# Second half's mixing matmuls: x and block diagonal split into high and low parts, three fp32r products for each fp32 one, one pair later

## The reference

```python
w = table[cond]                                   # 32 matrices of 32 x 32
y = einsum('bct,bcd->bdt', x, w)                  # mixing, per batch
h = silu(y @ w_gate) * (y @ w_up)                 # 1024 x 1024
h = keep_the_two_largest_of_each_four(abs(h), h)  # 2:4 sparsity, by magnitude
out = x + h @ w_down
```

## Time and profile before

| | us |
|---|---|
| median of three runs | 80.29 |
| profiled execution, its own time | 80.31 |
| its span | 78.4 |
| PE busy | 73.9 (94%) |
| DVE busy | 62.7 (80%) |
| ACT busy | 42.1 (54%) |
| share of PE in the chain that ended last | 94% |

### The profile page before, as it was taken

How to read it: one execution, slowest core, us unless ns; L and a number is a source line. 1 busy time by engine, 2 the same in 40 slices (tenths; PEclk the granted TensorE clock), 3 DMA queues, 4 the chain that set the end, 5 groups by cost and what they waited for, 6 DMA issues and landing times.

```text
span 78.4 us, 1027 instructions
## 1 busy us (share of the span) xinstructions
PE 73.9 (94%) x362; PEld 59.6 (76%) x362; DVE 62.7 (80%) x93; ACT 42.1 (54%) x62; POOL 8.1 (10%) x17
## 2 busy tenths in 40 slices
PE   3988999999999999999999999999999999999950
PEld 1328888888888888888888888888888888888840
DVE  1006884689889999599999979999999999994460
ACT  6122773799443465699897769798380402720000
POOL 3460000000000013000804000006200000000000
PEclk9999999999999999999999999999999999999999
DMA  0726979995910005900199990003994000003333
GB/s 1 273 95 168 286 234 318 302 418 180 410 67 0 0 0 98 169 0 0 36 196 199 184 192 8 4 0 67 201 180 88 0 0 0 8 0 140 135 134 126
DMA packets 4565, 9.64 MB, mean 123 GB/s; under 512 B 560, under 2 KB 2864, under 8 KB 4304
## 3 DMA queue, kind: packets, MB, share of 16 engines
q1 hardware_dynamic: 3488, 6.16, 23.0%
q0 software_dynamic: 928, 3.28, 21.9%
q10 hardware_dynamic: 144, 0.13, 0.5%
HBM read 5.38 MB, written 1.05 MB: 82 GB/s over the span
## 4 chain that ended last, share of the span: by engine, by line
PE 94%; issue 1%; DVE 1%
PE banks L579 52%; PE banks L621 28%; PE banks L541 6%; PE banks L564 4%; PE banks L591 3%; PE banks L550 1%; DVE gate_raw L455 1%; DVE warm L458 0%
## 5 line engine op out<-in xcount | busy, mean ns | idle before, releaser
L579 PE MATMUL banks<-y_hl,up_hl 128*128 128x512 f32 x96 | 24.2, 389 | 0.0
L621 PE MATMUL banks<-h_hl,down_hl 128*128 128x512 f32 (+1 forms) x102 | 22.0, 376 | 0.0
L579 PE MATMUL banks<-y_hl,gate_hl 128*128 128x512 f32 x84 | 21.4, 390 | 0.0
L621 PEld LDWEIGHTS banks<-h_hl,down_hl 128*128 128x128 f32 x102 | 18.5, 188 | 3.6
L579 PEld LDWEIGHTS banks<-y_hl,up_hl 128*128 128x128 f32 x96 | 18.0, 188 | 3.8
L579 PEld LDWEIGHTS banks<-y_hl,gate_hl 128*128 128x128 f32 x84 | 15.7, 188 | 3.2
L264 ACT ACTIVATE silu<-banks 128x512 f32<-128x512 f32 x16 | 9.6, 597 | 11.1 <-PE banks L579 10.8
L404 DVE TENSOR_TENSOR h<-banks,silu 128x512 f32<-128x512 f32 x12 | 8.2, 687 | 3.8 <-ACT silu L264 3.7
L285 ACT ACTIVATE h_hl<-h 128x1024 fp32r<-128x1024 f32 (+1 forms) x8 | 6.7, 842 | 3.9 <-DVE h L440 3.9
L440 DVE SCALAR_TENSOR_TENSOR h<-count,h 128x512 f32<-128x512 bf16 x12 | 7.9, 685 | 0.1
L271 ACT ACTIVATE x_sb<-h 128x512 f32<-128x512 f32 x8 | 4.9, 625 | 1.7 <-DVE h L404 1.7
(11 more groups left out here) (39 smaller groups left out, 66.7 us busy)
## 6 DMA issues: line engine op xcount, KB each, us to landing
h_hl<-h POOLq DMA_DIRECT2D x4, 512.0 KB, 6.1
x_sb<-in_x SPq DMA_DIRECT2D x2, 512.0 KB, 3.7
up_raw<-in_w_up SPq DMA_DIRECT2D x4, 256.0 KB, 4.3
down_raw<-in_w_down SPq DMA_DIRECT2D x1, 1024.0 KB, 7.6
gate_raw<-in_x_t SPq DMA_DIRECT2D x1, 1024.0 KB, 5.9
down_hl<-down_raw POOLq DMA_DIRECT2D x2, 512.0 KB, 4.9
gate_raw<-in_w_gate SPq DMA_DIRECT2D x3, 256.0 KB, 4.1
out<-gate_raw SPq DMA_DIRECT2D x3, 256.0 KB, 2.3
```

The lines of the kernel that those rows point to most:

```text
L579: last = nc.tensor.matmul(dst, w_hl[w][:, s, q, k, j], y_hl[:, m, half, k], start=i == 0, stop=i == len(terms) - 1)
L621: last = nc.tensor.matmul(bank[:, begin:end], down_hl[:, s, q, j, k * P:(k + 1) * P], h_hl[:, u, m, j, begin:end], start=(q, j, m, s) == f ...
```

## The change

The second half's x (128 x 1024) and its block diagonal (128 x 512) are each split into a high and a low fp32r part: ACT copies the high parts (`high_x`, `high_diagonal`), DVE subtracts to get the low parts (`low_x`, `low_diagonal`). They are kept in the part of `h_hl` that belongs to the last unit, which is written only near the end. `mixing_second_half` takes the place of `mixing(1)`: for each block and group three fp32r matmuls of 128 columns that add up in one bank, 24 in all where there were 8 of fp32. It stands ahead of pair 4, one pair later. `transpose_rows(1)` and `diagonal(SPANS[2])` move ahead of product(0) on DVE, and `high_y` and `low_y` of the second half stand behind `gate_silu(3)` and `product(3)`. The first half's mixing is as before, written as a function of its own.

```diff
--- before.py
+++ after.py
@@ -36,7 +36,7 @@
     RING = 3
     WARM_START = 12
     LAST = len(UNITS) - 1
-    MIX_PAIR = 3
+    MIX_PAIR = 4
     SENT = 2
 
 
@@ -76,6 +76,10 @@
         mix_w = h[:, 1, 1, 0:NG * D].rearrange("p (g o d) -> p g o d", o=1, d=D)
         mix_diag = h[:, 1, 2:4].rearrange("p m t -> p (m t)").rearrange(
             "p (g b d) -> p g b d", g=NG, b=NB)
+
+        last_h = h_hl[:, LAST].rearrange("p s m t -> p (s m t)")
+        x_hl = last_h[:, 0:2 * GH * T].rearrange("p (s g t) -> p s g t", s=2, g=GH)
+        diag_hl = last_h[:, 2 * GH * T:2 * GH * T + 2 * GH * P].rearrange("p (s g n) -> p s g n", s=2, g=GH)
         own_block = sb("own_block", [P, NB], f32)
         far = sb("far", [P, 4, TH], bf16)
         near = sb("near", [P, 2, TH], bf16)
@@ -117,6 +121,8 @@
         blocks_marked = sem("blocks_marked")
         transposed = sem("transposed")
         diag_done = sem("diag_done")
+        second_hi = sem("second_hi")
+        second_lo = sem("second_lo")
         mixed = sem("mixed")
         y_hi = sem("y_hi")
         y_lo = sem("y_lo")
@@ -177,6 +183,9 @@
         def parts_until(u, j):
             return sum(len(p) for p in PARTS[:u]) + 1 + max(i for i, p in enumerate(PARTS[u]) if p[0] <= j)
 
+        def second_diag():
+            return mix_diag[:, GH:NG].rearrange("p g b d -> p g (b d)")
+
         def raw_piece(i):
             q, w, k, end, j, j_end = PIECES[i]
             return raw_w[w][:, q, k:end].rearrange("p k (j g) -> p k j g", j=M)[:, :, j:j_end]
@@ -257,6 +266,14 @@
                 act.wait_ge(mixed, KT * half + end)
                 nc.scalar.activation(split_y(HI, half, k, end), mixed_y(half, k, end), ACT.Copy).then_inc(y_hi, 1)
 
+            def high_x():
+                act.wait_ge(x_in[1], 16)
+                nc.scalar.activation(x_hl[:, HI], x_sb[:, GH:NG], ACT.Copy).then_inc(second_hi, 1)
+
+            def high_diagonal():
+                act.wait_ge(diag_done, len(SPANS))
+                nc.scalar.activation(diag_hl[:, HI], second_diag(), ACT.Copy).then_inc(second_hi, 1)
+
             def gate_silu(n):
                 act.wait_ge(pair_done, n + 1)
                 if n >= 3:
@@ -298,15 +315,17 @@
                 high_weights(i)
             act.wait_ge(table_loaded, 1)
             gate_silu(0)
+            high_x()
             gate_silu(1)
+            high_diagonal()
             absolute(0)
             high_weights(LATER)
             gate_silu(2)
             absolute(1)
             high_weights(LATER + 1)
-            high_y(*Y_PIECES[KT])
             absolute(2)
             gate_silu(3)
+            high_y(*Y_PIECES[KT])
             absolute(3)
             gate_silu(4)
             gate_silu(5)
@@ -380,6 +399,18 @@
                 nc.vector.tensor_tensor(mix_diag[:, groups], mix_w[:, groups].broadcast_to(shape),
                                         mark.broadcast_to(shape), ALU.mult).then_inc(diag_done, 1)
 
+            def low_x():
+                dve.wait_ge(second_hi, 1)
+                dve.wait_ge(x_in[1], 16)
+                nc.vector.tensor_tensor(x_hl[:, LO], x_sb[:, GH:NG], x_hl[:, HI].bitcast(f32),
+                                        ALU.subtract).then_inc(second_lo, 1)
+
+            def low_diagonal():
+                dve.wait_ge(second_hi, 2)
+                dve.wait_ge(diag_done, len(SPANS))
+                nc.vector.tensor_tensor(diag_hl[:, LO], second_diag(), diag_hl[:, HI].bitcast(f32),
+                                        ALU.subtract).then_inc(second_lo, 1)
+
             def low_weights(i):
                 dve.wait_ge(w_hi, i + 1)
                 dve.wait_ge(*source(i))
@@ -467,16 +498,18 @@
                 low_y(k)
             for i in range(KT, LATER):
                 low_weights(i)
-            product(0)
-            product(1)
             transpose_rows(1)
             diagonal(SPANS[2])
+            product(0)
+            low_x()
+            product(1)
+            low_diagonal()
             low_weights(LATER)
             product(2)
             compare(0, 1)
             low_weights(LATER + 1)
+            product(3)
             low_y(KT)
-            product(3)
             compare(0, 2)
             compare(0, 3)
             product(4)
@@ -551,20 +584,27 @@
                                                 mix_w[rows, g, 0], start=True, stop=True)
                 last.then_inc(mixed, 1)
 
-            def mixing(half, first=0):
-                pe.wait_ge(x_in[half], 16)
-                if half > 0:
-                    pe.wait_ge(y_lo, KT * half)
-                for k in range(first, KT):
-                    for i in range(GH):
-                        g = half * GH + i
-                        span = [groups.start <= g < groups.stop for groups in SPANS].index(True)
-                        if k == first and g == SPANS[span].start:
-                            pe.wait_ge(diag_done, span + 1)
-                        last = nc.tensor.matmul(y_banks[:, k, i * P:(i + 1) * P],
-                                                x_sb[:, g, k * P:(k + 1) * P],
-                                                mix_diag[:, g].rearrange("p b d -> p (b d)"),
-                                                start=True, stop=True)
+            def mixing_second_piece():
+
+                for g in range(GH):
+                    span = [groups.start <= g < groups.stop for groups in SPANS].index(True)
+                    if g == SPANS[span].start:
+                        pe.wait_ge(diag_done, span + 1)
+                    last = nc.tensor.matmul(y_banks[:, 1, g * P:(g + 1) * P], x_sb[:, g, P:2 * P],
+                                            mix_diag[:, g].rearrange("p b d -> p (b d)"), start=True, stop=True)
+                last.then_inc(mixed, 1)
+
+            def mixing_second_half():
+
+                terms = ((HI, HI), (HI, LO), (LO, HI))
+                pe.wait_ge(second_lo, 2)
+                pe.wait_ge(second_hi, 2)
+                pe.wait_ge(y_lo, KT)
+                for k in range(KT):
+                    for g in range(GH):
+                        for s, m in terms:
+                            last = nc.tensor.matmul(y_banks[:, k, g * P:(g + 1) * P], x_hl[:, s, g, k * P:(k + 1) * P],
+                                                    diag_hl[:, m, g], start=(s, m) == terms[0], stop=(s, m) == terms[-1])
                     last.then_inc(mixed, 1)
 
             def split_product(dst, w, q, half, j):
@@ -628,11 +668,11 @@
             warm_up(WARM_START)
             pe.wait_ge(w_hi, pieces_until(0, 0, 0, 0))
             mixing_by_batch()
-            mixing(0, 1)
+            mixing_second_piece()
             first_gates()
             for n in range(PAIRS):
                 if n == MIX_PAIR:
-                    mixing(1)
+                    mixing_second_half()
                 gate_up(n)
             pe.wait_ge(y_lo, len(Y_PIECES))
             for u in range(NQ):
```

## The result

The changed kernel takes 81.24 us (median of six runs, 80.89 to 81.67) against 80.24 before (six runs). The ratio is 1.0116 with a 95% interval of 1.0077 to 1.0154, so 0.6 to 1.2 us slower; 81.15 was predicted. The profiled execution took 81.32 us, its span 79.5.

What follows compares the result with a forecast made beforehand. PE was taken as the bound. 24 slots of 0.112 (2.69 us) in place of 1.85 gave +0.84, all other parts nothing: 80.31 + 0.84 = 81.15 us; the case's own range was 81.0 to 81.4, the overall range 80.3 to 81.6 (82%).

Steps and rivals of the forecast that it cites:

- Price of a slot: Second half's mixing on PE: each fp32r matmul of 128 columns takes 0.112 us, 24 of them 2.69; forecast 68%.
- The two arguments: Mixing slot on PE: the weight load paces it at about 0.11 us, and fp32r loads last as long as fp32 ones.
- The stream's 0.065: Mixing on PE: streaming alone would take 0.065 us for 128 fp32r columns, the lower bound of a slot.
- The sum: Whole kernel: 80.31 + 0.84 = 81.15 us, only PE's mixing slots adding time.
- the entry wait: PE ahead of the old mixing: 0.06 us waiting for the diagonal from DVE, expected to go with the change.
- Split parts in time: ACT and DVE ahead of the mixing: low diagonal done near 17, PE there at 19.14; margin 2 us, no cost.
- The cost at the old place: Mixing left ahead of pair 3, at 16.42: without the later pair's cover, about 0.6 us.
- DVE's lag: DVE behind low y: product(4) 1.79 us later, 0.95 lost against PE, 0.12 left at product(7), no cost at the end.
- The slack at product(8): DVE's product(8) against the load of PE's pair 11: 0.08 us to spare, just enough, cost taken as 0.
- The rival in which DVE becomes the bound: At product(8): late copies or low y make pair 11 start late, 0.3 to 0.4 us, 81.5; 8%.
- Stream-paced slots: Rival for the mixing on PE: loads hide, 24 x 0.065 = 1.56 us, -0.29, total 80.0; 17%.
- full-price narrow matmuls: Rival for the mixing on PE: narrow fp32r matmuls cost 0.227 us like wide ones, +3.6, total 83.9; 7%.

Runs made afterwards that it cites:

- half load: Changed kernel, middle product using 64 of the 128 columns of x, so 8 of 24 loads half as long: 80.74 us, ratio 1.0049 to the kernel before.
- the old place: Changed kernel with the second half's mixing ahead of pair 3 instead of pair 4: median 82.22 us, ratio 1.0212 to the kernel before; profiled again, 81.50 us.
- two products: Changed kernel without the product of low x with the high diagonal, 16 fp32r matmuls instead of 24: 80.31 us, ratio 1.0002 to the kernel before.
- bf16 parts: Changed kernel with high and low parts of x and diagonal in bf16 instead of fp32r, still 24 matmuls: 79.87 us, ratio 0.9938 to the kernel before.
- splits made but not used: Changed kernel with the second half's mixing again 8 fp32 matmuls, the four splitting instructions still running: 80.36 us, ratio 0.9981 to the kernel before.

## Why the prediction was right

**Price of a slot.** Taken as 0.112 from the earlier trace rows, for want of a row of its own. Measured 0.112 from start to start, but for the first slot of 0.057: the mixing is 2.63 us, against 2.69 predicted. The two arguments hold one by one. The load is the limit (half of its columns, about half of the slot), and the fp32r load is as long as the fp32 one (188 to 192 in both). The stream's 0.065 for 128 columns, from the earlier trace rows, was about the right size for what lies under it: with a half load the slots came down to 0.06, so the stream is not more than that.

**The sum.** +0.84 was predicted: 2.69 less 1.85, with the entry wait inside. The profiles have 0.78 for that and 0.08 behind it, which no term of the sum had. The sum took all 24 slots as full; the first is 0.06 shorter and the first wide matmul behind them 0.06 longer, so the two errors cancel. Of the measured 0.93 by ratio, 0.86 is found in the profiles; the 0.07 left is within the interval.

**Split parts in time.** PE came to the mixing without a gap; low diagonal ended at 16.87 (predicted 17) and PE came at 19.41 (19.14 and the late start of that execution). The cost at the old place was put at 0.6, as a wait at the mixing. By the starts the mixing is 0.25 late, 0.35 with its slower run, in the execution in which x landed 4.0 after its issue, and 1.5 late where that took 5.2. The prediction took one landing time from the earlier trace rows and didn't allow for its spread.

**DVE's lag.** Product(4) was to be 1.79 late and was 27.50 - 25.52 = 1.98, of which 0.26 is the late start: 1.72. Product(7) was to have 0.12 of lag left; it shows none (33.86 - 32.73 = 1.13, PE's own shift being 1.12). The slack at product(8) was put at 0.08 and is 0.2, the same as before the change (39.06 + 0.69 = 39.75 against 40.06 - 0.11 = 39.95 from the earlier trace rows). It is little: DVE work added behind low y (1.14 us) shows at PE nearly in full, and a weight piece that landed late cost 0.2 us in one execution. That DVE stands at low y until the mixing is through was right (2.21 us), and it means that a shorter mixing frees DVE earlier too: the kernels with two products and with bf16 parts kept the 0.2. The rival in which DVE becomes the bound was real: one more instruction behind low y brings it about.

**The rivals.** Stream-paced slots (0.065) and full-price narrow matmuls (0.227) are both excluded for fp32r. The bf16 slots, 0.056, are short enough for the first, which no run tells from a load that is short enough. The Trainium skill's "TensorE: Matmul & The Clock Gate", Back-to-back issue gap, has about 81 ns for 128 columns in a stream with loads; this case has 111 for fp32 and fp32r and 56 for bf16, and neither is 81. The Trainium skill's count of four passes for fp32 ("FP8 and Floating Point Precision", TensorE Precision Notes) would by itself give a gain from 32 to 24; the trace shows two records and two loads for each fp32 matmul, and it is the loads, 16 against 24, that the time follows.

## What to carry to other kernels

Count weight loads, not passes, where fp32 or fp32r matmuls are narrower than about 256 columns and each has its own load of 128: at 128 columns three fp32r products in place of one fp32 matmul cost half as much again, because one fp32 matmul loads twice and the three products three times. (How the two compare at 512 columns no run here shows: the kernel has no fp32 matmul of that width.) If the precision allows it, bf16 parts halve the slot. When work is added to an engine that is not the bound, look for the place where it waits for the bound engine: what was added ahead of that wait cost nothing here (3.6 us on ACT and DVE), and 1.14 us added behind it cost 0.9.

## What the runs showed of the hardware that was not expected

- After an interruption of the stream of wide matmuls (the narrow ones, or a wait) the next ones are slower for 1 to 2 us. With the change the steps from pair half to pair half are 1.45 and 1.38 us at 22.03 and 23.48, then 1.36 or 1.37; before the change 1.47 at 18.19, then 1.36. By the single records some of the wide matmuls there are 0.230 to 0.236 apart instead of 0.227. What it comes from was not tried.
- The twelve warm-up matmuls take 4.17 to 5.30 us in executions of nearly the same program, by when they go over from 0.427 to 0.216 apart. Up to 5.11 (splits made but not used) this is hidden by what the mixing waits for anyway: its first matmul stands at 6.25 there and at 6.23 in the kernel before. 5.30 is 0.26 us at the end in the changed kernel. In the bf16 kernel's profile, where the mixing by batch is slow as well (1.35 us for 1.09), the pairs' first products are 0.57 late.
- A doubling of the moving columns from 128 to 256 costs 0.008 us for a matmul with fp32r operands and its own load (0.112 to 0.120).
